# A four-stage fp32 model kernel: index columns made on POOL ahead of unlimited y scatters, and four smaller moves around it

## The reference

```python
x = x + time_mix(layer_norm(x), w_rvk, w_out, time_decay, time_first)
x = x + moe(layer_norm(x))      # router of 64 experts, 4 chosen per token, plus one shared FFN for all tokens
x = x + retention(layer_norm(x), w_qk, w_vg, w_o, ...)   # per head decay, group norm, gate
x = x + moe(layer_norm(x))      # the same weights a second time
```

## Time and profile before

| | us |
|---|---|
| runs of the kernel before | 1674.37, 1681.01, 1685.75 (median 1681.01) |
| the profiled execution | 1671.73 |
| its span in the profile | 1670.0 |

### The profile page before, as it was taken

How to read it: one execution, slowest core, us unless ns; L and a number is a source line. 1 busy time by engine, 2 the same in 40 slices (tenths; PEclk the granted TensorE clock), 3 DMA queues, 4 the chain that set the end, 5 groups by cost and what they waited for, 6 DMA issues and landing times. The chain is left out here.

```text
span 1670.0 us, 24490 instructions
## 1 busy us (share of the span) xinstructions
PE 1315.8 (79%) x7416; PEld 900.8 (54%) x7416; DVE 1091.6 (65%) x2773; ACT 688.9 (41%) x1468; POOL 921.0 (55%) x1066
## 2 busy tenths in 40 slices
PE   6787569992799978898989987599936877777775
PEld 3344435651688864464656655356625655555533
DVE  5899787771366654475868667477634665665568
ACT  6999311210566652335151522222104655545420
POOL 4999357665555545765656161376643655655510
PEclk9899579996899998999999988799978988888878
DMA  9900432224688865212121010722346444443178
GB/s 359 390 1 0 170 147 94 101 101 126 219 270 283 270 222 167 72 51 62 36 67 35 20 37 17 277 101 92 104 126 183 146 143 150 154 137 103 28 264 277
DMA packets 109396, 233.82 MB, mean 140 GB/s; under 512 B 21543, under 2 KB 43470, under 8 KB 108756
## 3 DMA queue, kind: packets, MB, share of 16 engines
q1 hardware_dynamic: 81076, 164.03, 29.2%
q0 software_dynamic: 27648, 68.23, 12.0%
q10 hardware_dynamic: 544, 0.00, 0.0%
HBM read 125.44 MB, written 115.11 MB: 144 GB/s over the span
## 5 line engine op out<-in xcount | busy, mean ns | idle before, releaser
L936 POOL DMA_INDIRECT slots_x<-arena,slot x240 | 242.3, 1010 | 168.1 <-DMA slots_x<-arena,slot 127.7
L1305 POOL DMA_INDIRECT pairs_y<-arena x192 | 189.8, 989 | 157.7 <-DVE arena L1376 87.9
L1368 DVE TENSOR_TENSOR arena<-arena,moe_narrow 64x128 f32<-64x128 f32 x384 | 111.6, 291 | 205.4 <-ACT arena L1270 171.9
L1222 PE MATMUL moe_narrow<-arena 128*128 128x128 f32 x1536 | 224.8, 293 | 12.1 <-DVE arena L1368 9.0
L1211 PE MATMUL moe_narrow<-ident,arena 128*128 128x128 f32 x768 | 134.9, 304 | 120.6 <-DMA arena<-slots_x 59.5
L1222 PEld LDWEIGHTS moe_narrow<-arena 128*128 128x128 f32 x1536 | 204.5, 207 | 22.3 <-issue 20.4
L1264 ACT ACTIVATE arena<-moe_narrow 128x512 f32<-128x512 f32 x192 | 114.7, 597 | 186.9 <-remote 95.6
L734 PE MATMUL moe_wide<-arena 128*128 128x512 f32 x384 | 183.0, 623 | 9.9 <-issue 8.3
L1211 PEld LDWEIGHTS moe_narrow<-ident,arena 128*128 128x128 f32 x768 | 92.0, 153 | 172.7 <-issue 169.1
L456 POOL DMA_INDIRECT arena<-slots_y,slot x128 | 128.9, 1007 | 93.3 <-DMA arena<-slots_y,slot 60.4
L1376 DVE COPY arena<-moe_wide 128x512 f32<-128x512 f32 x192 | 128.3, 689 | 21.4 <-remote 8.8
(11 more groups left out here) (333 smaller groups left out, 2443.5 us busy)
## 6 DMA issues: line engine op xcount, KB each, us to landing
arena<-slots_x SPq DMA_DIRECT2D x192, 264.0 KB, 3.8
slots_x<-arena SPq DMA_DIRECT2D x48, 528.0 KB, 15.7
slots_y<-arena SPq DMA_DIRECT2D x96, 256.0 KB, 3.3
arena<-w_gu SPq DMA_DIRECT2D x2, 8192.0 KB, 29.2
arena<-pairs_y SPq DMA_DIRECT2D x32, 512.0 KB, 4.4
residual<-x SPq DMA_DIRECT2D x8, 512.0 KB, 7.9
arena<-sw_gu SPq DMA_DIRECT2D x4, 1024.0 KB, 4.9
slots_x<-arena,slot POOLq DMA_INDIRECT x256
```

What stands on the lines that cost most here:

```text
L936: pool.indirect_dma_start(out=x_slots, in_=xn[:, t, :], in_offset=None, out_offset=bass.IndirectOffsetOnAxis(ap=slot[:, t, i:i + 1], axis=0))\
L1222: last = pe.matmul(h_ps[n % 2][:, j * P:(j + 1) * P], weights[:, n % 3, j, h, :], xt[:, n % XTRING, (j * KH + h) * P:(j * KH + h + 1) * P] ...
L1305: pool.indirect_dma_start(out=slots.y_of, in_=ytile[:, n % YRING, j, :], in_offset=None, bounds_check=slots.pairs - 1, oob_is_err=False, o ...
L1368: product = dve.tensor_tensor(ht[j * F:(j + 1) * F, n % HTRING, cols], sig[F:2 * F, n % 2, cols], h_ps[n % 2][F:2 * F, cols], ALU.mult)
```

## The change

There are five parts.

(A) In the second layer's expert stage the wait for pair n - 2's scatters is gone. The DVE now leaves the target as a float in `target_of`, and POOL adds NOWHERE and converts to integer itself, one 128x1 column ahead of each scatter, with a wait for its own result (`link`).
(B) `FirstBlocks.scatter` has one scatter in flight, not two.
(C) In retention the 32 gathers of batch 0 (`apart=b > 0`) have no limit on how many are in flight.
(D) FB of moe2 is 7 instead of 6: one more block's shared FFN in the route, one less in the closing sum.
(E) The first two blocks of moe1 get their statistics, powers and, for block 0, the normalised tiles at the end of time_mix (DVE, POOL, ACT); moe1 starts without them, and its POOL makes `power(2, 3)` before the scatters and `power(3, 5)` after the first eight. ACT's table load moves into time_mix too.

```diff
@@ experts_gpsimd, moe2 (A)
+                columns = Chain(pool, exp_sem("column_steps"))
                 for n in range(NP):
                     if n % 2 == 0:
                         pool.wait_ge(exp_sem("targets"), n // 2 + 1)
                     pool.wait_ge(exp_sem("y_kept"), n + 1)
-                    if n >= 2:
-                        pool.wait_ge(exp_sem(f"y_out{(n - 2) % YRING}"), Y_LANDED * ((n - 2) // YRING + 1))
                     for j in range(2):
+                        column = slice(2 * n + j, 2 * n + j + 1)
+                        columns.link(pool.tensor_scalar(goes_to[:, column], target_of[:, column], float(slots.NOWHERE), None,
+                                                        ALU.add))
                         pool.indirect_dma_start(
...
@@ targets, on the DVE (A)
-                steps.link(dve.tensor_reduce(target, hits, AX_X, ALU.add))
-                steps.link(dve.tensor_scalar(goes_to[:, 2 * n:2 * n + 4], target, float(slots.NOWHERE), None, ALU.add))
+                steps.link(dve.tensor_reduce(target_of[:, 2 * n:2 * n + 4], hits, AX_X, ALU.add))
@@ FirstBlocks.scatter (B)
-            if at >= 2:
-                pool.wait_ge(self.landed[at % 2], 16 * (at // 2))
+            if at:
+                pool.wait_ge(self.landed[(at - 1) % 2], 16 * ((at + 1) // 2))
@@ retention, gather (C)
-                    choices.gather(pool, TB * b + t, apart=True)
+                    choices.gather(pool, TB * b + t, apart=b > 0)
@@ second layer and closing sum (D)
-        experts(nc, k, "moe2", 2, True, 6, k.res.shape[1], router_w, ...
+        experts(nc, k, "moe2", 2, True, 7, k.res.shape[1], router_w, ...
-                if 9 <= pair <= 11:
-                    add_down((pair - 8) // 2, (pair - 8) % 2)
+                if pair == 8:
+                    add_down(0, 1)
@@ time_mix: ACT, POOL, DVE at its end (E)
+            act.preload_act_table(ACT.Silu)
+            act.wait_ge(sem("lead_ready"), 1)
+            for j in range(BLK):
+                act.activation(lead_xn[:, j, 0:C], k.res[:, j, :], ACT.Identity, ...
...
+            for g in range(k.LEAD):
+                pool.wait_ge(sem("lead_var"), g + 1)
+                steps.link(pool.tensor_tensor(k.lead_rstd[:, g], k.lead_rstd[:, g], k.minus_half[:, 0:BLK], ALU.pow))
...
+                if n == UNITS + 1:
+                    for g in range(k.LEAD):
+                        lead_statistics(g)
@@ moe1 start, POOL (E)
-                power(0, 1)
-                power(1, 2)
-                power(2, 5)
+                pool.sem_inc(sem("moments_ready"), LEAD)
+                power(LEAD, LEAD + 1)
...
                     if n == 0 and j == BLK // 2:
                         pool.wait_ge(sem("slots_ready"), 2)
+                        power(LEAD + 1, LEAD + 3)
@@ moe1 start, DVE (E)
-                statistics(0)
-                statistics(1)
-                normalise_first(2)
-                for n in range(2, 5):
-                    statistics(n)
+                dve.sem_inc(sem("var_ready"), LEAD)
+                statistics(2)
                 choose(0)
                 slots_of(0)
-                statistics(5)
+                statistics(3)
+                statistics(4)
                 choose(1)
```

More of the change, by code:

```diff
@@ L357, in statistics, with lead_statistics @@
                 dve.sem_inc(sem("var_ready"), 1)
+            def lead_statistics(g):
+                dve.wait_ge(sem("op_read"), 2 * (g + 1))
+                for j in range(BLK):
+                    steps.step(dve.bn_stats(stats[:, g, j, :], k.res[:, BLK * g + j, :]))
+                steps.settled()
+                for j in range(BLK):
+                    steps.step(dve.bn_aggr(moments[:, g, j, :], stats[:, g, j, :]))
+                steps.settled()
+                steps.step(dve.tensor_scalar(k.lead_rstd[:, g], moments[:, g, :, 1], EPS, None, ALU.add))
+                steps.link(dve.tensor_scalar(k.lead_offset[:, g], moments[:, g, :, 0], -1.0, None, ALU.mult))
+                dve.sem_inc(sem("lead_var"), 1)
             def differences(n):
@@ L581, in experts @@
     sht = arena.take(HRING, N)
-    assert arena.at <= (first.TOP if first else k.ZERO_AT)
+    assert arena.at <= (first.TOP if first else k.ZERO_AT - 8 * k.LEAD)
     arena.at = at_experts
@@ L619, in experts @@
     SENT = first.SENT if first else 0
+    LEAD = 0 if first else k.LEAD
     order = [DONE] + list(range(DONE)) + list(range(DONE + 1, NB))
@@ L806, in route_scalar, with normalise @@
         def route_scalar(act):
-            act.preload_act_table(ACT.Silu)
-            def normalise(n, tiles=BLK):
+            if first:
+                act.preload_act_table(ACT.Silu)
+            def normalise(n):
                 act.wait_ge(sem("moments_ready"), n + 1)
-                shifts, scales = (first.offset, first.rstd) if n < SEEN else (offset, rstd)
-                for j in range(tiles):
+                shifts, scales = (first.offset, first.rstd) if n < SEEN else \
+                    (k.lead_offset, k.lead_rstd) if n < LEAD else (offset, rstd)
+                for j in range(BLK):
                     act.activation(xn[:, BLK * n + j, 0:D], k.res[:, BLK * n + j, :], ACT.Identity,
@@ L849, in route_scalar @@
             else:
-                normalise(0, 2)
+                act.sem_inc(sem("xn_done"), BLK)
                 keep_transposes(0, 0)
@@ L1109, in route_vector @@
                 pick_gates(1)
-                statistics(6)
-                statistics(7)
+                for n in range(5, NB):
+                    statistics(n)
             for n in range(FB):
@@ L2763, in program @@
         first = retention(nc, k, w_qk, w_vg, w_o, b_q, b_k, b_vg, b_o, gn_w, gn_b, gamma, sw_gu, sw_d, router_w, router_bias, x.shape[0])
-        experts(nc, k, "moe2", 2, True, 6, k.res.shape[1], router_w, router_bias, w_gu, w_d, sw_gu, sw_d, out=out, first=first)
+        experts(nc, k, "moe2", 2, True, 7, k.res.shape[1], router_w, router_bias, w_gu, w_d, sw_gu, sw_d, out=out, first=first)
 def kernel(**inputs):
```

27 lines of the change are left out of this document (16 added, 11 removed).

## The result

| | kernel before | changed kernel |
|---|---|---|
| median of 4 runs, us | 1678.49 | 1769.95 |
| ratio | 1 | 1.0504 (95% interval 1.0458 to 1.055) |
| span of the profiled execution | 1670.0 | 1769.2 |

The change makes the kernel 5% slower; 1667 with a range of 1636 to 1701 was forecast. The page of the changed kernel: busy time, the chain that ended last by engine and by line, and two groups that answer to the earlier trace rows and to the DVE's copy of y.

The account below looks back on a forecast made before the run. moe2's expert stage was taken as bound by a chain of waits, not an engine. Terms -3 + 2.3 - 1.5 - 8.5 + 0.8 - 5.1 + 1 = -14.0 took 1671.7 to 1657.7, scaled to a 1667 us median; range 1636 to 1701.

Parts of the forecast that it names:

- the cost of the added column: moe2's y scatters: column, gap and scatter cost about 1.57 us, against 1.28 for scatters back to back.
- 0 for the 88 pairs in the middle: moe2's y stage: added columns hide in POOL's waiting time, costing 0; if nothing hid them, +56 us.
- Rival 1: moe2's y stage: added columns make POOL the bound, at 1.95 us a scatter; net +24, median 1705; chance 0.18.
- The limit, worth 4 us: moe2's y scatters: the removed wait for pair n - 2's scatters held back only 4.0 us in the 300 shown.
- The tail, + 2.3: End of moe2's y stage: the last eight scatters have no cover, so their added columns cost 2.3 us.
- C, - 8.5: Retention's start: gathers without a limit bring the power 13 us earlier and save 8.5; bounds 4.3 to 13.
- B, - 1.5, bounds - 4 to + 3: Retention's 16 early scatters, one in flight: fewer unnamed DVE waits, 1.5 us saved; up to 4 gained or 3 lost.
- D, + 0.8 and - 5.1: moe2: one more block's FFN lengthens the route by 0.8 us; the closing sum gets 5.1 shorter.
- E, + 1: moe1's start: earlier transposes gain 1 us, the power among the scatters costs 1.9; net +1, bounds -4 to +3.
- Rival 2: moe2's y stage: wider scatter spacing halves the unnamed stops, -45; net -59, median 1622; chance 0.17.

Follow-up runs that it names:

- The kernel pair with and without a wait: Kernel before without the limit, plus a 128x1 POOL instruction into a spare column ahead of each scatter: unwaited 1614.3 us, ratio 0.9962; waited for 1742.8 us, ratio 1.0797.
- on record: The study's main measurement of the changed kernel against the kernel before: 1769.95 against 1678.49 us, ratio 1.0504.
- quiet runs: Sets of runs in which no engine waits for an event the profile can't name; the kernel before took about 1617 us.
- with stops: Sets of runs where ACT's y-stage eviction waits for unnamed events, except in the changed kernel; kernel before about 1685 us, 1678 in the main measurement.
- a limit of three: Kernel before with scatters waiting for those of pair n - 3 instead of n - 2: 1692.4 against 1683.0 us, ratio 1.0083.

## Why the prediction was wrong

- **The failed step: the cost of the added column.** I took 0.19 + 0.30 + 1.07 = 1.57 us from the IOTA ahead of the first early scatter. Measured: 0.23 + 0.78 + 1.06 and 0.04 between, 2.10. The term that was mis-sized is the gap between column and scatter, 0.30 there and 0.78 here. The kernel pair with and without a wait shows that the wait is what costs. The IOTA is waited for too, so the row was of the right pattern and still not of the right price; why its gap is 0.30 stays open. The nearer row was there: a y scatter for which POOL stood still starts 0.77 us after the DVE's copy.
- **"0 for the 88 pairs in the middle"** fell with it. The point from which it decides was given rightly, 1.75 us a scatter; 2.10 lies beyond it. Rival 1 was the case that came, at 0.18. It took 1.95 as its price and so 1705 us; with 2.10 x 191 = 401 us even its own sum would have been + 75, and + 91 was measured, as the mean over the stage is 416.9 / 191 = 2.18. I had given it two reasons, and the second, a link dearer than the IOTA's, is the one that came. The first was a column held up by the DVE's copies, with the rule of the Trainium skill (GPSIMD Engine Reference, Key points) on the shared interfaces. The trace doesn't bear that out as the cause: the column takes 0.23 us (median; the longest 0.55), and the DVE's copies run beside it at an unchanged 0.689 us.
- **The limit, worth 4 us.** Near enough on record, where the limit held scatters back for 6.7 us of the y stage. In quiet runs it is worth 46; with stops nothing was gained by taking it away (C, D, E without it 1.0029, a limit of three 1.0083).
- **The tail, + 2.3**: part of the + 91 now.
- **C, - 8.5.** Right in sign in quiet runs, where C alone gave 14.5 us (10.7 to 19.1 by its interval), past my bound of 13 for POOL's whole gain. On record retention's part up to the early scatters was 9.0 us longer (+ 8.6 against - 0.4). With stops unlimited gathers come with late results of PE, in each of the three kernels that have them and in none of the five that don't, and C gains nothing. The 9.0 us themselves are no more than five kernels without C differ by in that part (360.8 to 369.6).
- **B, - 1.5, bounds - 4 to + 3.** Both signs came. On record this stretch is 3.9 us shorter (+ 4.7 against + 8.6), and the DVE's unnamed waits of the earlier trace rows are gone from it. The scatters took 41.4 us from first to last, near the 43 forecast, but the group norm's power was not in time with 3 to 4 us to spare: it stands right behind them at 1037.32, with no idle time. In quiet runs this stretch is 4 us longer with B.
- **D, + 0.8 and - 5.1.** On record the route is 4.5 us longer (from + 4.7 to + 9.2) and the end, from the last y scatter on, 1.9 shorter. Alone and quiet it is 0.9963, some 6 us, near my - 4.3.
- **E, + 1.** The first scatter came 4.9 us earlier, the first gather 0.4: the third scatter still waited 6.57 us for landings, to 216.41. The mechanism was right, and the size near nothing (alone and quiet 0.9986).
- **Rival 2**, shrinking stops, was right as a mechanism: they go in the changed kernel's y stage. It gained nothing, since at 2.10 us POOL alone is slower than the stops were.

The loss is A's: + 91 us of + 99.2 on record, and 1.0741 of 1.0715 in quiet runs.

## What to carry to other kernels

Work that is "hidden in idle time" in a chain of 192 steps has to be priced as a chain: instruction, wait and start, each with its own row. The row of a wait must be of the same two instructions: a wait for an IOTA, 0.30 us, was no measure of a wait for a 128x1 column, 0.78. Here, making an index on POOL and scattering by it one after the other costs 0.8 us a scatter over what a bare scatter does; make indices in groups, or one step ahead, or on another engine. And the releaser that a page names is the last one that fits by its time. Where a ring lets one engine run ahead of another, count the tiles: a limit's worth is read from the chain that ended last, or measured by taking it away.

## What the runs showed that I had not expected

- The same kernel took 1617 us in some sets of runs and 1683 in others, on one and the same chip too, and each set was steady within 1 to 2%. What differs is late results of PE (by the code, PE is what the unnamed waits are for) while indirect DMAs run densely; their cause stays open. A comparison of two kernels can turn with it: the missing limit with C, D and E is 0.966 in one case (with B) and 1.003 in the other (without B).
- Spacing helps with stops: an instruction that does nothing, ahead of each scatter, makes the kernel 2.1% faster there (0.9788) with the limit gone, and leaves it at 0.9962 when quiet. Two kernels were measured both ways; this one is under 1 in both, the changed one in neither. Whether spacing alone would do it, with the limit kept, wasn't measured.
- The idle time of POOL between a 128x1 column and an indirect DMA is 0.78 us if POOL waits for that column, 0.16 if it waits only for the one before, and 0.17 without a wait. The same 0.77 us lies between the end of the DVE's copy and a scatter that stood still for it, and 0.30 between an IOTA and a scatter that waits for it.
